# Windowed attention: the row maxima subtracted by VectorE on the way out of PSUM, and the mask written by eight 64x32 tiles

## The reference, cut to what matters

```python
for i in range(DEPTH):                                   # 6
    x = attn_layer(shift_tokens(x), Wqkv[i], q_scale[i], k_scale[i], Wo[i]) + x
    x = ffn_layer(shift_tokens(x), ln_g[i], ln_b[i], W1[i], b1[i], W2[i], b2[i]) + x

# local_attention: 16 heads of 64, windows of 32 queries, each sees its own window and the one before (64 keys)
mask = (it < jb) | (it > jb + w) | (jb == -1)
sim  = jnp.einsum('bhwie,bhwje->bhwij', bq, bk2) * QK_SCALE
sim  = jnp.where(mask, -jnp.finfo(sim.dtype).max, sim)
attn = jax.nn.softmax(sim, -1)
out  = jnp.einsum('bhwij,bhwje->bhwie', attn, bv2)
```

## Time and profile before

| | |
|---|---|
| median of 3 runs | 2299.03 us |
| profiled execution | 2296.43 us, span 2294.6 us |
| PE busy | 2073.0 us, 90% |
| DVE busy | 1664.1 us, 73% |
| ACT busy | 1058.1 us, 46% |
| POOL busy | 700.5 us, 31% |
| mean granted clock of PE | 0.963 |
| one undisturbed iteration | 36.4 us |

### The profile page before, as it was taken

The page is one execution under the profiler, slowest core; times in us unless marked ns, Lnnn a source line. Parts: engine busy times, 40 slices in busy tenths (PEclk is TensorE's granted clock), DMA queues, the critical chain, the costliest instruction groups (busy, mean ns, idle before and its releaser), DMA issues.

```text
span 2294.6 us, 83156 instructions
## 1 busy us (share of the span) xinstructions
PE 2073.0 (90%) x34896; PEld 1326.2 (58%) x34896; DVE 1664.1 (73%) x3316; ACT 1058.1 (46%) x1911; POOL 700.5 (31%) x974
## 2 busy tenths in 40 slices
PE   6989895799989899989999899999899998999996
PEld 2333332466656666656667566666566665666664
DVE  5555645687867778777878687878678777878783
ACT  2333332255544445544545454545345554545553
POOL 0000002343433334333434243434333433434330
PEclk9999998899999999989999899999899998999997
DMA  1000101464554555555555454645555555656551
GB/s 55 5 9 5 51 0 21 73 94 76 85 104 76 85 81 82 81 98 91 89 81 85 97 92 76 94 69 89 92 100 79 81 77 99 96 85 87 83 75 36
DMA packets 72465, 168.23 MB, mean 73 GB/s; under 512 B 16496, under 2 KB 23408, under 8 KB 71408
## 3 DMA queue, kind: packets, MB, share of 16 engines
q0 software_dynamic: 36864, 100.71, 33.6%
q1 hardware_dynamic: 35456, 65.41, 11.1%
HBM read 20.30 MB, written 1.05 MB: 9 GB/s over the span
## 4 chain that ended last, share of the span: by engine, by line
PE 62%; DVE 22%; issue 7%; DMA 4%; ACT 2%; SPq 1%; POOL 0%; DVEq 0%; POOLq 0%; ACTq 0%
PE ps L934 8%; PE ps L901 7%; PE ps L823 6%; PE ps L990 5%; PE ps L1010 5%; DVE big L724 5%; PE ps L1046 5%; DVE big L727 4%; PE ps L1003 4%; PE ps L954 4%; DVE mneg L740 3%; PE ps L1035 2%; PE ps L924 2%; DVE den L744 2%; PE ps L844 2%
## 5 line engine op out<-in xcount | busy, mean ns | idle before, releaser
L402 POOL DMA_DIRECT2D big<-big x768 | 604.1, 1233 | 703.1 <-DVE big L727 663.9
L901 PE MATMUL ps<-big,wn_sb 128*128 128x256 f32 x1536 | 416.9, 400 | 56.6 <-DVE big L727 20.3
L470 ACT ACTIVATE big<-ps 128x512 f32<-128x512 f32 x384 | 229.8, 598 | 459.1 <-PE ps L901 459.0
L901 PEld LDWEIGHTS ps<-big,wn_sb 128*128 128x128 f32 x1536 | 275.3, 194 | 141.1 <-DVE big L727 71.0
L724 DVE TENSOR_TENSOR big<-ps,tab 128x512 f32<-128x512 f32 x384 | 255.2, 675 | 61.2 <-ACT big L470 61.2
L735 DVE TENSOR_TENSOR big<-big,ps 128x512 f32<-128x512 f32 x384 | 249.5, 681 | 64.4 <-PE ps L924 52.9
L740 DVE TENSOR_REDUCE mneg<-ps 128x8 bf16<-128x512 f32 x192 | 127.0, 683 | 222.5 <-PE ps L954 222.3
L481 ACT ACTIVATE big<-ps 128x512 f32<-128x512 f32 x192 | 114.7, 597 | 323.6 <-PE ps L934 323.6
L727 DVE TENSOR_TENSOR big<-ps,tab 128x512 f32<-128x512 f32 x384 | 257.1, 680 | 0.0
L1046 PE MATMUL ps<-big,wo_sb 128*128 128x256 f32 x768 | 215.3, 383 | 0.1
L934 PE MATMUL ps<-wn_sb,big 128*64 128x512 f32 x768 | 182.1, 616 | 4.1 <-DVE big L735 0.8
(11 more groups left out here) (147 smaller groups left out, 3052.5 us busy)
## 6 DMA issues: line engine op xcount, KB each, us to landing
big<-big POOLq DMA_DIRECT2D x768, 128.0 KB, 4.3
big<-big SPq DMA_DIRECT2D x96, 256.0 KB, 4.0
big<-big SPq DMA_DIRECT2D x96, 192.0 KB, 4.4
wn_sb<-in_wn SPq DMA_DIRECT2D x6, 1536.0 KB, 7.6
...
```

What stands on the lines that cost most here:

```text
L402: eng.dma_start(rot[to:to + 32, at:at + 4, :], src[32 * r:32 * r + 32], accum_op=ALU.add).then_inc(added[g], 16)
L470: eng.activation(sq[:, two, :], ps[:, i % 2, :].rearrange("p (a t) -> p a t", a=2), ACT.Square).then_inc(sq_d, 1)
L901: mm = eng.matmul(ps[:, k % 2, a * T:a * T + T], wn_sb[:, u * P:u * P + P], sT, start=True, stop=True)
```

## The change

- PE: `M0` to `M3` are gone. The mask is laid by eight products on 64x32 tiles (four tiles of columns by two of rows, each 512 columns wide) in place of two on the whole array. `s_go` counts the start of each `S`.
- DVE: `X` keeps the maxima in f32, and a new step `D` (four in an iteration) reads the bank, subtracts the maxima and writes the difference to SBUF.
- ACT: `x` is one exp over a chunk, 1024 columns, from SBUF to SBUF in place; there are two in an iteration, where there were four of 512 columns out of PSUM.
- What waited for `ex_d` to have the banks free (`S1`, `W0`) waits for `sub_d`.
- All three tables are written anew.

```diff
         PE_PLAN = [(x_[0], int(x_[1:])) for x_ in """
-            S0 k0 M0 M1 k1 F1 T0 k2 F2 k3 S1 g0 g1 k4 k5 M2 M3 T1 k6 T2 k7 g2 g3 W0 W1 T3 F4 U0 W2 W3 U1 O0 O1
-            F5 R0 O2 R1 U2 O3 R2 U3 F6 R3 O4 R4 O5 F7 R5 R6 O6 O7 R7 V0 V1 V2 V3""".split()]
+            S0 k0 k1 F1 S1 F2 k2 g0 k3 T0 T1 k4 g1 W0 k5 W1 k6 T2 k7 F4 g2 g3 W2 T3 F5 U0 U1 W3 O0 O1 O2 O3 F6
+            R0 R1 F7 U2 R2 U3 R3 O4 R4 O5 R5 R6 O6 O7 R7 V0 V1 V2 V3""".split()]
         ACT_PLAN = [(x_[0], int(x_[1:])) for x_ in """
-            s0 x0 x1 s1 F1 s2 s3 F2 s4 t0 s5 x2 x3 s6 s7 t1 t2 n0 t3 u0 F4 u1 F5 u2 u3 v0 v1 v2 v3""".split()]
+            s0 s1 F1 s2 x0 F2 s3 t0 t1 s4 s5 x1 s6 s7 t2 F4 n0 t3 u0 u1 F5 u2 u3 v0 v1 v2 v3""".split()]
         DVE_PLAN = [(x_[0], int(x_[1:])) for x_ in """
-            X0 X1 c0 d0 F1 c1 d1 Z0 F2 c2 c3 f0 d2 d3 X2 f1 X3 c4 d4 c5 d5 f2 f3 f4 Z1 c6 n0 d6 Y0 N0 N1 N2 N3
-            N4 c7 N5 d7 N6 Y1 H0 H1 F5 H2 F6 H3 H4 H5 H6 H7 e0 F7""".split()]
+            X0 X1 D0 D1 F1 c0 d0 c1 X2 d1 F2 X3 D2 c2 d2 f0 D3 f1 c3 d3 f2 c4 d4 f3 c5 d5 f4 Z0 c6 Y0 n0 Z1 N0
+            c7 N1 d6 N2 d7 N3 F5 N4 N5 N6 F6 Y1 H0 H1 H2 H3 H4 H5 H6 H7 F7 e0""".split()]
...
                     if kind == "x":
-                        c, r = divmod(i, 2)
-                        eng.wait_ge(sm_d, it * 4 + (i + 1 - 4))
-                        eng.activation(pr_[:, c, :, KW * r:KW * r + KW], ps[:, 5 + r, :].rearrange("p (g k) -> p g k", g=8),
-                                       ACT.Exp).then_inc(ex_d, 1)
+                        eng.wait_ge(sub_d, it * 4 + (2 * i + 2 - 4))
+                        chunk = pr_[:, i, :, :]
+                        eng.activation(chunk, chunk, ACT.Exp).then_inc(ex_d, 1)
...
+                    if kind == "D":
+                        c, r = divmod(i, 2)
+                        eng.wait_ge(max_d, it * 4 + (i + 1 - 4))
+                        eng.tensor_tensor(pr_[:, c, :, KW * r:KW * r + KW], ps[:, 5 + r, :].rearrange("p (g k) -> p g k", g=8),
+                                          top[:, c, r, :].rearrange("p (g k) -> p g k", k=1).to_broadcast((P, 8, KW)),
+                                          ALU.subtract).then_inc(sub_d, 1)
...
-                        eng.wait_ge(ex_d, it * 4 + (2 - 4))
+                        eng.wait_ge(sub_d, it * 4 + (2 - 4))
                         eng.wait_ge(hat_d, it * PAIRS)
-                    for r in range(2):
-                        eng.matmul(ps[:, 5 + r, :], ident_b[:, :], mask_cb[:, :].rearrange("p (a k) -> p a k", a=1).to_broadcast((P, 4, P)),
-                                   start=True, stop=False, skip_group_check=True)
+                    eng.sem_inc(s_go, 1)
+                    for w in range(4):
+                        for r in range(2):
+                            rows = slice(64 * r, 64 * r + 64)
+                            eng.matmul(ps[WIN * w:WIN * w + WIN, 5 + r, :], id32[rows, :],
+                                       mask_cb[rows, min(w, 1):min(w, 1) + 1, :].to_broadcast((64, 4, P)), start=True, stop=False,
+                                       skip_group_check=True)
...
-                def less_maxima(i):
-                    c, r = divmod(i, 2)
-                    eng.wait_ge(max_d, it * 4 + (i + 1 - 4))
-                    eng.matmul(ps[:, 5 + r, :], ident_b[:, :], mneg[:, c, r, :].rearrange("p (g k) -> p g k", k=1).to_broadcast((P, 8, KW)),
-                               start=False, stop=True, skip_group_check=True).then_inc(sm_d, 1)
```

More of the change, by code:

```diff
@@ L60, in shape_constants @@
     rot = np.stack([8.0 * both(cq), 8.0 * both(sq)[other], both(ck), both(sk)[other]], 1).astype(f)
-    q, k = np.arange(P)[:, None] % WIN, np.arange(2 * WIN)[None, :]
+    q, k = np.arange(WIN)[:, None], np.arange(KW)[None, :]
     seen = np.where(k < WIN, k >= q, k - WIN <= q)
-    first = seen & ((np.arange(P)[:, None] >= WIN) | (k >= WIN))
-    mask_c = np.concatenate([np.where(first, 0.0, MASKED), np.where(seen, 0.0, MASKED)], 1).astype(f)
+    one = np.where(seen, 0.0, MASKED)
+    first = np.where(seen & (k >= WIN), 0.0, MASKED)
+    rows = lambda a: np.concatenate([a, np.zeros_like(a)] * 2, 0)
+    mask_c = rows(np.concatenate([first, one, one, one], 1)).astype(f)
+    id32 = rows(np.eye(WIN)).astype(f)
     p = np.arange(P)
@@ L115, in gated_flamingo @@
         onehot = sb("onehot", [H, H, P], BF16)
[L116 to L117 removed]
+        id32 = sb("id32", [P, WIN], BF16)
+        mask_cb = sb("mask_cb", [P, 2, P], BF16)
         zeros = sb("zeros", [P, 1, T])
@@ L197, in gated_flamingo @@
         mrow = sb("mrow", [H, T], BF16)
-        mneg = sb("mneg", [P, 2, 2, 8], BF16)
+        top = sb("top", [P, 2, 2, 8])
         den = sb("den", [P, 2, 2 * 8])
@@ L227, in gated_flamingo @@
                              "y_d", "r_d", "rb", "hat_d"))
-        sc_d, max_d, sm_d, ex_d, den_d, rinv_d, pt_d, ptev, ov_d, on_d, ot_d, oev, wo_d, x_d, w_go, vf_free = (
-            sem(n) for n in ("sc_d", "max_d", "sm_d", "ex_d", "den_d", "rinv_d", "pt_d", "ptev", "ov_d", "on_d", "ot_d", "oev",
-                             "wo_d", "x_d", "w_go", "vf_free"))
+        sc_d, max_d, sub_d, ex_d, den_d, rinv_d, pt_d, ptev, ov_d, on_d, ot_d, oev, wo_d, x_d, w_go, s_go, vf_free = (
+            sem(n) for n in ("sc_d", "max_d", "sub_d", "ex_d", "den_d", "rinv_d", "pt_d", "ptev", "ov_d", "on_d", "ot_d", "oev",
+                             "wo_d", "x_d", "w_go", "s_go", "vf_free"))
         chain, nchain, nmid = sem("chain"), sem("nchain"), sem("nmid")
@@ L365, in _ @@
             eng.wait_ge(s_const, 16 * 4)
-            eng.tensor_copy(ident_b[:, :], ident).then_inc(cast, 1)
-            eng.tensor_copy(mask_cb[:, :], part["mask_c"]).then_inc(cast, 1)
+            eng.tensor_copy(id32[:, :], part["id32"]).then_inc(cast, 1)
+            eng.tensor_copy(mask_cb[:, :, :].rearrange("p a k -> p (a k)"), part["mask_c"]).then_inc(cast, 1)
             eng.tensor_copy(onehot[:, :, :], stage_hot[0:H]).then_inc(cast, 1)
@@ L708, in body @@
                     eng.wait_ge(fvc, l if isinstance(b, int) else l + 1)
-                for kind, i in share(DVE_PLAN, A, Bh, F, "cdnNH", "XZYe", "Ff"):
+                for kind, i in share(DVE_PLAN, A, Bh, F, "cdnNH", "XDZYe", "Ff"):
                     if kind == "n":
@@ L739, in body @@
                         eng.wait_ge(sc_d, it * 2 + (c - 1))
-                        eng.tensor_reduce(mneg[:, c, r, :], ps[:, 5 + r, :].rearrange("p (g k) -> p g k", g=8), AX.X, ALU.max,
-                                          negate=True).then_inc(max_d, 1)
+                        eng.tensor_reduce(top[:, c, r, :], ps[:, 5 + r, :].rearrange("p (g k) -> p g k", g=8), AX.X,
+                                          ALU.max).then_inc(max_d, 1)
+                    if kind == "D":
[4 more added lines that the diff above has]
+                                          ALU.subtract).then_inc(sub_d, 1)
                     if kind == "Z":
-                        eng.wait_ge(ex_d, it * 4 + (2 * i + 2 - 4))
+                        eng.wait_ge(ex_d, it * 2 + (i - 1))
                         eng.tensor_reduce(den[:, i, :], pr_[:, i, :, :].rearrange("p g (r k) -> p (g r) k", r=2), AX.X,
@@ L1048, in project_out @@
                         mm.then_inc(wo_d, 1)
-                steps = {"k": project, "g": head_sums, "V": values, "R": spread, "S": score, "M": less_maxima, "T": turn_weights,
+                steps = {"k": project, "g": head_sums, "V": values, "R": spread, "S": score, "T": turn_weights,
                          "W": weigh, "U": turn_outputs, "O": project_out, "F": ffn}
-                for kind, i in share(PE_PLAN, A, Bh, F, "kgRV", "SMTWUO", "F"):
+                for kind, i in share(PE_PLAN, A, Bh, F, "kgRV", "STWUO", "F"):
                     steps[kind](i)
```

8 lines of the change are left out of this document (4 added, 4 removed).

## The result

The changed kernel takes **2450.3 us** (median of 4 runs, 2443.7 to 2451.9), the kernel before 2297.0 in the same comparison (2294.7 to 2303.8): a ratio of **1.066**, with an interval of 1.063 to 1.069. It is slower by 153 us. Forecast were 2480 us, between 2400 and 2555.

A forecast was written before the change was run, and what follows sets the result against it. PE was taken to set the pace, with DVE only 2.4 us from taking over as the bound. 2296.4 + 156 (table loads) + 25 (clock) = 2477, plus 2.6 for the median: 2480 us, range 2400 to 2555.

The forecast's parts named there:

- the seam: Stretch from H7's end to X0's start, 5.12 us in every iteration before, forecast at 4.9 after the change.
- PE's relief: PE's work per iteration falls by 1.5 us: 1.0 from the dropped M steps, 0.24 per S from the mask.
- the floor of 36.2: DVE's work around an iteration without a single wait: 36.2 us, against 36.39 for the iteration before.
- `D`: Four new DVE reads of PSUM per iteration, 683 ns each, 0.60 us of path, 2.4 us in all.
- The exps: On ACT, four of 611 ns become two of about 1.05 us, hidden in idle time at no cost.
- The table loads: On ACT, five per iteration instead of two, 1283 ns each; iteration 39.8 us, 3.4 more, 156 us in all.
- the chain: From n0 on DVE through ACT's loads, Ln and Exp to N0; DVE stands 2.8 us, N0 starting at 22.3.
- The clock: PE's gap of 2.0 to 2.8 us before U1 lowers its clock in half the iterations: 46 x 0.55 = 25 us.
- This holds in the 46 iterations with part F: 46 x 3.4 = 156 us: The 3.4 us that table loads add to one iteration, applied to all 46 iterations with part F: 156 us.
- The drain: Rival: each load on ACT also brings a drain, 190 us on top, 2670 us; 2 in 100.
- The loads hide: Rival: two loads fall into ACT's idle time, iteration 36.4 us, no change, 2299 us; 4 in 100.
- PE's relief decides: Rival: D takes 0.3 us of DVE's path, loads hidden, a gain of 62 us, 2237 us; 5 in 100.

The follow-up runs named there:

- e2: Changed kernel with Square in place of Gelu, so no table load in the loop (Gelu left out): 2307.0 us, 1.0048.
- f3: e2 with two extra unused row sums on DVE between Z1 and N0: 2374.1 us, 1.033.
- e3: Kernel before with Square in place of Gelu, so no table load in the loop (Gelu left out): 2297.8 us, 1.0008.
- f4: Changed kernel with fourteen unused bf16 products on PE ahead of U1, in the gap where PE waits for t3: 2440.5 us, 1.062.
- e1: Changed kernel with the table set holding Ln and Exp loaded before n0, four loads per iteration instead of five: 2366.0 us, 1.032.

## Why the prediction was right

- **What bounds it.** Right. With PE at 35.7 of 36.4 us and DVE with 2.4 us to spare before the seam, PE's relief could not be cashed. Without loads (e2) the steady iteration is 36.66 us against the floor of 36.2 and small waits. The floor was a little high: e2's 36.66 hold 0.57 us of wait at `F6` and 0.32 at `H7`, which leaves 35.8, and f3 found 0.7 us of room.
- **PE's relief.** The sign is right, the size open. By e2 against e3 PE's busy time fell by 0.6 us in an iteration (35.00 against 35.58), not by 1.5. Ends of matmuls are modelled, and in e3 PE hardly idles; no run here separates what the `M` steps gave. The mask gave 0.31 us per `S`; I took 0.24. It needed one pass and not eight (0.23 us), so the tiles do run side by side.
- **`D`.** Right: 682 ns of busy time, 0.60 us of path. From 1252.78 the four reads `X0 X1 D0 D1` take 2.4 us in all, the half of it for `D`. DVE's work grew by 2.2 us (31.91 against 29.74). Of the 153 us this and all else but the loads made 9 or 10.
- **The exps.** 1050 ns where 1.05 us was estimated; `T` waits for them 2.6 us in the whole program.
- **The table loads.** 236 loads ran, two more than I had counted (the two at the start were left out of the 234), at 1283 ns, and the chain is right. From `X0` (1252.78) `n0` ends at 17.9 us (18.1 in the working), Ln starts at 19.9 (20.0), Exp at 21.7 (21.8), `N0` at 22.1 (22.3), and DVE stands 2.75 (2.8). The seam takes 4.62 us (4.9). An iteration without a fall of the clock takes 39.58 to 39.85 us: forecast were 39.8. Here the working has a slip. Laid end to end it was 0.5 us too long for the kernel before (36.9 against 36.39), and of 40.0 it took off 0.2 and called that nearly as much; with the whole 0.5 it would have said 39.5, which is closer to the 39.58 of f4, and 143 us in place of 156. The rows that are counted from 1252.78, in an iteration with a fall:

```profile
1270.31 0.41 DVE L715 TENSOR_SCALAR big<-ps 128x256 f32<-128x256 f32 x1
...
1272.71 0.42 ACT L478 ACTIVATE big<-big 128x256 f32<-128x256 f32 x1
...
1274.44 0.42 ACT L480 ACTIVATE big<-big 128x256 f32<-128x256 f32 x1
...
1274.89 0.43 DVE L665 TENSOR_TENSOR big<-big 128x256 f32<-128x256 f32 x1 [2.75 <-ACT big L480]
...
1288.19 0.69 DVE L738 TENSOR_TENSOR big<-big,ps 128x512 f32<-128x512 f32 x1 [0.32 <-PE ps L933]
```

`H7` ends at 36.1 us after `X0`, where 35.1 was worked out; the difference is the fall of the clock, which the working had as a term of its own. DVE stands 1.08 us at `F6` for PE there; in f4, where the clock stays up, it doesn't, and `H7` ends at 34.9.
- **The clock.** The price of a fall, 1.1 us, is right (f4, and e1). How often it falls was put at half of the iterations, 23 of 46. It is 25 of the 30 lengths away from layer starts, while those at the starts gain few new ones. Falls of 1.1 us in 25 lengths are 28 us, where the working had 25: the size of the term is right by luck. From the mean granted clock (0.944 here, 0.963 before) the lost work is 0.056 x 2447 = 137 us against 0.037 x 2295 = 85: 52 us more work lost, which is 31 stretches of 3.4 us at half rate; only a part of it is time.
- **What failed: "This holds in the 46 iterations with part F: 46 x 3.4 = 156 us".** It doesn't hold at a layer's start. A layer's start is here the length that crosses into it and the two behind. Of the first 45 lengths from `n0` to `n0`, 28 lie away from it and grew by 3.80 us each (3.95 with the clock in the working), but the 17 at layer starts (two in the first, three in each of the others) grew by 1.87. Over these 45 the working's 3.95 make 178 us and measured are 138: of the 40 too many, 17 x (3.95 - 1.87) = 35 stand at layer starts. Behind them, in the last two lengths and at the program's end, the changed kernel lost 15 us (6.4 and 8.5), for which the working had 4 left. So the whole was only 28 us too high (181 forecast, 153 measured): a part of the error was covered by luck. Such a start in windows, three lengths from `n0` to `n0`, the changed kernel first, where it grew by 7.6 us:

```profile
1351.77:1487.07 135.30, 111.52 (x2082) 75.89 (x2082) 99.40 (x188) 68.75 (x106) 44.90 (x61) 0.94 0.50 89
```

```profile
1285.08:1412.75 127.67, 111.15 (x2083) 76.27 (x2070) 93.11 (x175) 57.90 (x102) 44.77 (x61) 0.95 0.54 94
```

There PE stood idle for 16.5 of 127.7 us already, and the clock was at 0.95, and is at 0.94 after: one fall more, not three. DVE's waits in these two stretches show what hid the new one. `N0` waits 8.5 us there, the full 2.8 each time, and the wait at `F5` is new with 1.6. But DVE's waits in sum have hardly grown, from 33.5 to 35.7 us: `X` waits 12.6 us for PE instead of 15.3, `H` 1.0 instead of 4.3, `F6` 0.9 instead of 1.9, `Y` no longer for 0.8, and the first `c` and `F1`, which have changed places, 8.0 instead of 8.5. What is left of the growth is mostly DVE's own work, 6.3 us more. So waits on other things took in most of the new one. The working rested on one undisturbed iteration and multiplied it by all.
- **The drain.** The case in which each load brings a drain gave 2670 us. Behind a load the next ACTIVATE starts at once (1232.47 + 1.28 = 1233.75, and 1233.77), as the earlier trace rows had it, and ahead of one the ACTIVATE before it ends 0.02 us earlier (1229.88 + 0.84, and 1230.74). Taking one load out (e1) shortened `N0`'s wait by 1.26 us. The Trainium skill, "ScalarE: Activation LUTs", section "What ACT_TABLE_LOAD costs", has about 2.66 us for each switch; the traces disagree with that, and agree with its 1283 ns for the load.
- **The other rivals.** "The loads hide" and "PE's relief decides" need `N0` within 19.5 and 19 us of `X0`; it starts at 22.1. Even with the loads out of the way (e2) the kernel gains nothing, so the 62 us of the second were not there: `D` costs its 0.60 us of path.
